# The last chunk's attention goes to layer 2's gates by a product of values and input weights

## The chip, the cores and the metric

One of the eight cores of a Trainium2 chip runs the kernel. The metric is the device time of one execution in microseconds; before the change it is 414.52 us (median of 3 runs, 414.26 to 414.95).

## The reference, cut to what matters

`x` is 16 x 128 x 128 (batch, time, features), `cond` 16 x 128. Two LSTM layers run over time with an attention without softmax between them and a feed-forward block behind them:

```python
hs = lstm(x, cond, Wx1, Wh1, b1)            # 128 steps; gates i, f, o sigmoid, g tanh
theta, phi, v = hs @ W_theta.T, hs @ W_phi.T, hs @ W_g.T
x = x + ((theta @ phi.T) / sqrt(128)) @ v   # over all 128 times of a batch row, no softmax
hs2 = lstm(x, cond, Wx2, Wh2, b2)           # 128 steps
x = x + relu(hs2 @ W1 + b1f) @ W2 + b2f
```

A step of an LSTM is `a = x_t @ Wx + b + h @ Wh`, `c = f*c + i*g`, `h = o*tanh(c)`. Layer 2's first step needs the attention's sum over all times, so it needs layer 1's last `h`.

## The kernel before, in words

The batch of 16 and 8 times make a chunk of 128 columns; there are 16 chunks (`NCH`), and a loop pass holds two (`STEPS` = 16 steps, `CH` = 8). Everything is kept with features on partitions. Each engine has its own instruction stream, written out by hand, with semaphores between; nothing is scheduled by a planner.

A step (function `step` of each engine): TensorE multiplies the last `h` (`ring`) with the f weights in f32 into `fbank` (L413), and the f16 high and low parts of `h` with two f16 parts of the g, i and o weights into `gbank`, `ibank` and `bankV` (L407). ScalarE makes the gates (f L818, g L825, i L828, o L833) and `tanh(c)` (L836). VectorE makes `f*c` (L1003), the scan that adds `i*g` (L1006), the o gate times a unit (L1013), then `h` as f32 into `ring` (L1016), its high part (L1018) and its low part (L1021). The input's and the bias's part of the gates stands in the same PSUM columns already: ScalarE copies the bias there (`seed`, L852) and TensorE adds `Wx` times the chunk (`project_gate`, L372) a chunk ahead, beside the steps. `bias_gate` (L367) does both for f.

Beside the steps each engine works off a list by the step's number (`beside1` in layer 1; in layer 2's first 16 steps the blocks `if s == ...`). In layer 1, `row_products` makes, from the 8 new times, keys' and values' rows (`rows`), SP's queue moves them by DMA into an order by batch row (`rows_t`, L277), and the attention of the first two chunks of queries is summed in `bankV` (`score_products` L477, mask by `keep_scores` L1028, `early_attention` L482). `fill` (L386) issues matmuls of no use that keep TensorE busy. The queries of chunks 2 to 15 come after layer 1: `outer_pair` (L610) makes keys times values of two batch rows, `attend_pair` (L623) multiplies it with the hidden states `hist_late`, and `late_x2` (L1109) adds x.

Between the layers: with the last `h` TensorE makes the score product, the values' rows and the keys' rows; ScalarE copies them; `early_attention` completes chunk 0, VectorE adds x (`early_x2`, L1034) to give `x2T[:, 0]`, and four projections give layer 2's gates of its first 8 steps. `initial` (L391) has added `h0` times `Wh2` for step 0 during layer 1's last chunk. Steps of layer 2 then follow, the first 16 written out on all engines, the rest in loops. TensorE and ScalarE have layer 1's last 16 steps written out; VectorE has them in its loop. All engines take their instructions in order, so a wait holds up everything behind it on that engine.

## Time and profile before

| | us |
|---|---|
| median of 3 runs | 414.52 |
| profiled execution | 414.66 |
| its span, first to last instruction | 412.7 |
| TensorE matmul busy | 392.8 (95%) |
| VectorE busy | 273.1 (66%) |
| ScalarE busy | 206.7 (50%) |
| TensorE weight load busy | 293.2 (71%) |
| chain of waits: TensorE, VectorE, ScalarE, issue | 68%, 17%, 9%, 4% of the span |

The profile is of one execution. PE is TensorE's matmul row, PEld its weight loads, DVE VectorE, ACT ScalarE, SPq the queue of SyncE. PE's busy share holds the fills, and matmuls overlap; it doesn't say that TensorE is the bound. The granted clock was 1.00 (2.4 GHz) over the whole span.

### The profile page before, as it was taken

The page shows a single profiled execution, that of the slowest core. Times are in us where ns is not written, and L with a number is a line of the kernel's source. Part 1 is how long each engine was busy: PE and PEld are TensorE (multiplying, and loading weights), DVE is VectorE, ACT ScalarE, POOL GpSimd, SP SyncE. Part 2 cuts the span into 40 slices and gives each one's busy share as a digit, 9 for nine tenths or more (in the row PEclk, how much of TensorE's full clock was granted, in tenths as well). Part 3 has the DMA queues.
Part 4 walks back from the last instruction along what each step waited for, and adds up shares of the span by engine and source line. Part 5 has one row for each costly group of instructions (what it writes and reads, how often), then busy time and mean ns, then how long its engine had stood idle before and what let it go on. Part 6 is the DMA issues. An engine that isn't in the chain of part 4 may idle for free.

```text
span 412.7 us, 14901 instructions
## 1 busy us (share of the span) xinstructions
PE 392.8 (95%) x4979; PEld 293.2 (71%) x4979; DVE 273.1 (66%) x1697; ACT 206.7 (50%) x1451; POOL 8.1 (2%) x20
## 2 busy tenths in 40 slices
PE   8999999999999999999999999999999999999996
PEld 6777666677666677666689877777777777777775
DVE  5676666665666666666668776666677666676664
ACT  3666555555544555544556444444444444444442
POOL 7000000000000000000000000000000000000000
PEclk9999999999999999999999999999999999999999
DMA  5111011111011111010000100000000000000000
GB/s 159 39 21 21 6 17 19 19 19 19 2 17 19 19 19 18 3 17 14 15 15 2 27 20 6 20 19 19 19 6 13 19 19 19 19 9 10 19 19 13
DMA packets 11697, 8.20 MB, mean 20 GB/s; under 512 B 1098, under 2 KB 11130, under 8 KB 11675
## 3 DMA queue, kind: packets, MB, share of 16 engines
q1 hardware_dynamic: 10842, 6.17, 7.5%
q0 software_dynamic: 544, 1.23, 1.0%
q10 hardware_dynamic: 288, 0.52, 0.4%
q8 instruction: 13, 0.21, 0.2%
q14 instruction: 10, 0.07, 0.1%
HBM read 2.87 MB, written 1.05 MB: 9 GB/s over the span
## 4 chain that ended last, share of the span: by engine, by line
PE 68%; DVE 17%; ACT 9%; issue 4%; DVEq 0%; ACTq 0%
PE fbank L413 22%; PE fbank L386 9%; DVE cell L1006 6%; DVE ring L1016 5%; ACT fgate L818 5%; DVE scan L1003 5%; ACT cell L836 5%; PE bankU L630 4%; PE bankV L407 4%; PE ibank L407 4%; PE gbank L407 3%; PE bankV L482 3%; PE bankY L637 2%; PE bankY L477 2%; PE bankU L515 2%
## 5 line engine op out<-in xcount | busy, mean ns | idle before, releaser
L413 PEld LDWEIGHTS fbank<-ring,whf 128*128 128x128 f32 x508 | 75.5, 188 | 77.9 <-DVE ring L1016 74.1
L386 PE MATMUL fbank<-warm_w 128*128 128x384 bf16 x537 | 125.2, 325 | 0.1
L818 ACT ACTIVATE fgate<-fbank 128x16 f32<-128x16 f32 x254 | 46.8, 184 | 139.3 <-PE fbank L413 138.9
L413 PE MATMUL fbank<-ring,whf 128*128 128x16 f32 x508 | 99.8, 272 | 15.1 <-DVE ring L1016 8.8
L1003 DVE TENSOR_TENSOR scan<-fgate,cell 128x16 f32<-128x16 f32 x254 | 43.7, 172 | 70.5 <-ACT fgate L818 61.1
L1016 DVE TENSOR_TENSOR ring<-cell,ogate_h 128x16 f32<-128x16 f32 x256 | 44.5, 174 | 41.7 <-ACT cell L836 41.3
L836 ACT ACTIVATE cell<-cell 128x16 f32<-128x16 f32 x256 | 43.0, 168 | 54.1 <-DVE cell L1006 53.9
L1006 DVE TENSOR_TENSOR_SCAN cell<-scan 128x32 f32<-128x32 f32 x256 | 59.4, 232 | 10.0 <-ACT scan L828 1.3
L407 PE MATMUL ibank<-h_hi,wh_parts 128*128 128x16 f16 x508 | 62.0, 169 | 0.0
L407 PEld LDWEIGHTS gbank<-h_hi,wh_parts 128*128 128x128 f16 x508 | 52.2, 137 | 0.0
L1021 DVE TENSOR_TENSOR h_lo<-ring,h_hi 128x16 f16<-128x16 f32 x256 | 44.9, 175 | 8.7
L386 PEld LDWEIGHTS fbank<-warm_w 128*128 128x128 bf16 x537 | 42.4, 97 | 10.0 <-issue 0.7
L407 PE MATMUL gbank<-h_hi,wh_parts 128*128 128x16 f16 x508 | 49.3, 169 | 0.0
L407 PE MATMUL gbank<-h_lo,wh_parts 128*128 128x16 f16 x508 | 49.3, 169 | 0.0
L407 PE MATMUL bankV<-h_hi,wh_parts 128*128 128x16 f16 x508 | 49.3, 169 | 0.0
L407 PE MATMUL bankV<-h_lo,wh_parts 128*128 128x16 f16 x508 | 49.3, 169 | 0.0
L407 PE MATMUL ibank<-h_lo,wh_parts 128*128 128x16 f16 x508 | 49.3, 169 | 0.0
L825 ACT ACTIVATE scan<-gbank 128x16 f32<-128x16 f32 x256 | 47.6, 186 | 1.2 <-PE gbank L372 1.2
L833 ACT ACTIVATE ogate<-bankV 128x16 f32<-128x16 f32 x256 | 47.1, 184 | 0.3 <-PE bankV L372 0.3
L828 ACT ACTIVATE scan<-ibank 128x16 f32<-128x16 f32 x256 | 46.4, 181 | 0.1
L407 PEld LDWEIGHTS ibank<-h_hi,wh_parts 128*128 128x128 f16 x508 | 43.4, 95 | 0.0
L1018 DVE TENSOR_TENSOR h_hi<-cell,ogate_h 128x16 f16<-128x16 f32 x256 | 42.0, 164 | 0.0
(189 smaller groups left out, 603.1 us busy)
## 6 DMA issues: line engine op xcount, KB each, us to landing
rows_t<-rows SPq DMA_DIRECT2D x16, 128.0 KB
x_rows<-in_x_dram SPq DMA_DIRECT2D x17, 64.0 KB
out_dram<-y_sb SPq DMA_DIRECT2D x16, 64.0 KB
xres<-x2T SPq DMA_DIRECT2D x15, 64.0 KB, 1.9
xin<-x2T SPq DMA_DIRECT2D x14, 64.0 KB, 1.8
w<-in_L_ffn_W_dram POOLq DMA_DIRECT2D x2, 256.0 KB, 4.0
wh<-in_L_cond_Wh_dram ACTq DMA_DIRECT2D x1, 256.0 KB, 3.0
wx<-in_L_cond_Wx_dram ACTq DMA_DIRECT2D x1, 256.0 KB, 3.5
```

The source lines that it names most:

```text
L386: nc.tensor.matmul(fbank[1 - p][:, P:4 * P], warm_w[:], warm_three, start=False, stop=True, skip_group_check=True)
L407: last = nc.tensor.matmul(step_out(p, t, g), wh_parts[layer][:, part, gate_cols(g)], h[:, (s - 1) % STEPS, :], start=False, stop=True, ski ...
L413: nc.tensor.matmul(step_out(p, t, GF), whf[layer][:], ring[:, (s - 1) % STEPS, :], start=False, stop=True, skip_group_check=True).then_inc ...
L818: nc.scalar.activation(fgate[:], fbank[p][:, NB * t:NB * t + NB], ACT.Sigmoid, scale=1.0 / Z_UNIT).then_inc(f_done[layer], 1)
L825: nc.scalar.activation(g_slots, shared_cols(p, GG)[:, NB * t:NB * t + NB], ACT.Tanh, scale=1.0 / Z_UNIT).then_inc(scan_inputs[layer], 1)
L828: nc.scalar.activation(i_slots, shared_cols(p, GI)[:, NB * t:NB * t + NB], ACT.Sigmoid, scale=1.0 / Z_UNIT).then_inc(scan_inputs[layer], 1)
L833: nc.scalar.activation(ogate[:], shared_cols(p, GO)[:, NB * t:NB * t + NB], ACT.Sigmoid, scale=1.0 / Z_UNIT).then_inc(o_done[layer], 1)
L836: nc.scalar.activation(tanhc, c_psum, ACT.Tanh).then_inc(h_inputs[layer], 1)
L1003: nc.vector.tensor_tensor(out=fc_slots, in0=fgate[:], in1=c_psum, op=ALU.mult).then_inc(scan_inputs[layer], 1)
L1006: nc.vector.tensor_tensor_scan(out=c_scan, data0=scan_mul, data1=scan_add, initial=0.0, op0=ALU.mult, op1=ALU.add).then_inc(c_ready[layer], 1)
L1016: nc.vector.tensor_tensor(out=ring[:, s, :], in0=tanhc, in1=ogate_h[:], op=ALU.mult).then_inc(h_ready[layer], 1)
L1021: nc.vector.tensor_tensor(out=h_lo[:, s, :], in0=ring[:, s, :], in1=h_hi[:, s, :], op=ALU.subtract).then_inc(lo_ready[layer], 1)
```

## The change

The sum of attention over chunks 0 to 14 for chunk 0's queries, with x, is formed beside step 14 of the last pass (`x2_base`, VectorE) and projected to g, i, f beside step 15 and to o after it. The last chunk's part no longer goes through the attention's output: beside steps 1 and 9 TensorE multiplies `wg_rows` with `Wx2` (`value_w`, scaled by VectorE after steps 3 and 11), and after the last step it makes `last_keys` times `value_w` for each gate (`gate_rows`, copied by ScalarE for g and o, by VectorE for i and f) and multiplies that with the masked scores straight into the gates (`attend_gate`). The complete `x2T[:, 0]`, the last chunk's rows and their DMA, the addition for chunk 1, the outer products, the late attention, and with them projections and feed-forward products move to later steps of layer 2. VectorE's last pass of layer 1 is written out.

```diff
@@ sync
-                sp.wait_ge(rows_kept, c + 3 + (c == NCH - 1))
+                sp.wait_ge(rows_kept, c + 3)
@@ tensor: step
+                if base_read:
+                    pe.wait_ge(base_kept, 1)
                 passes(h_hi, GO, (0, 1))
@@ tensor: beside1
+                before_last = isinstance(i, int) and i == ITER - 1
+                if before_last and t == 1:
+                    nc.tensor.matmul(bankY[:, 2 * P:4 * P], wg_rows[:], wx[1][:, 2 * P * p:2 * P * p + 2 * P],
+                                     start=True, stop=True).then_inc(value_w_ready, 1)
+                if before_last and t == 4:
+                    pe.wait_ge(value_w_kept, p + 1)
...
+                elif before_last and t == 1:
+                    fill(p, 1)
+                elif last and t >= 6:
+                    fill(p, 1)
                 else:
                     fill(p, FILL1[t])
                 if last:
                     fill(p, {2: 1, 3: 1, 4: 1}.get(t, 0))
-                    due = {3: (GG,), 5: (GI,), 7: (GO,)}
+                    due = {3: (GG,), 5: (GI,), 6: (GO,)}
...
-                    early_attention(rows[:, p, D:2 * D], 0, 0, 2 * P)
+                    attended = early_attention(rows[:, p, D:2 * D], 0, 0, 2 * P)
+                    if last:
+                        attended.then_inc(base_ready, 1)
+                if last and t == 7:
+                    project_gate(1, 0, GF, x2_base[:])
+                    fill(p, 1)
+                    pe.wait_ge(o_done[0], T)
+                    project_gate(1, 0, GG, x2_base[:])
+                    project_gate(1, 0, GI, x2_base[:])
@@ tensor: between the layers
+            def rows_of(g, out):
+                nc.tensor.matmul(out, last_keys, value_w[:, gate_cols(g)], start=True, stop=True
+                                 ).then_inc(gate_rows_ready, 1)
+            def attend_gate(g):
+                return nc.tensor.matmul(gate_out(0, g), gate_rows[:, g, :], scores[:, 0:P], start=False, stop=True,
+                                        skip_group_check=True)
             score_products(0, last_keys, 0, P).then_inc(scores_ready, 1)
-            nc.tensor.matmul(bankU[:, D:2 * D], last_keys, proj[:, 1, :], start=True, stop=True
-                             ).then_inc(rows_ready, 1)
-            nc.tensor.matmul(fbank[1][:, 0:D], last_keys, proj[:, 0, :], start=True, stop=True).then_inc(rows_ready, 1)
-            fill(1, 1)
-            pe.wait_ge(rows_kept, NCH + 2)
+            rows_of(GG, bankU[:, 0:P])
+            rows_of(GI, fbank[1][:, 0:P])
+            project_gate(1, 0, GO, x2_base[:])
             pe.wait_ge(scores_kept, NCH + 1)
-            early_attention(rows[:, 0, D:2 * D], 0, 0, P).then_inc(early_attn_ready, 1)
-            pe.wait_ge(rows_kept, NCH + 3)
+            rows_of(GO, bankY[:, 0:P])
+            pe.wait_ge(gate_rows_act, 1)
+            attend_gate(GG).then_inc(g_ready[1], 1)
+            rows_of(GF, bankU[:, 0:P])
+            pe.wait_ge(gate_rows_dve, 1)
+            attend_gate(GI).then_inc(i_ready[1], 1)
+            pe.wait_ge(gate_rows_act, 2)
+            attend_gate(GO).then_inc(o_ready[1], 1)
             bias_gate(1, 1, GF)
-            fill(1, 1)
-            pe.wait_ge(x2_first, 1)
-            project_gate(1, 0, GG, x2T[:, 0, :]).then_inc(g_ready[1], 1)
...
+            pe.wait_ge(gate_rows_dve, 2)
+            attend_gate(GF).then_inc(f_ready[1], 1)
@@ tensor: layer 2, first 16 steps
-                    step(1, s, s, x2_read=2 if s == 2 else None,
+                    step(1, s, s, x2_read={2: 1, 4: 2}.get(s),
                 if s == 0:
+                    row_products(1, bankY)
+                if s == 1:
                     nc.tensor.matmul(bankU[:, 0:D], hist[:, 0, :], proj[:, 1, :], start=True, stop=True
                                      ).then_inc(rows0_ready, 1)
+                    fill(0, 2)
+                    pe.wait_ge(rows_kept, NCH + 2)
+                    pe.wait_ge(o_done[1], 2)
+                    early_attention(rows[:, 0, D:2 * D], 0, 0, P).then_inc(early_attn_ready, 1)
+                if s == 2:
                     score_products(0, last_keys, P, P)
                     score_products(P, hist[:, 0, :], P, P).then_inc(scores_ready, 1)
+                    fill(0, 3)
+                if s == 3:
                     pe.wait_ge(rows0_kept, 1)
+                    pe.wait_ge(rows_moved[1], 16 * (ITER + 1))
+                    pe.wait_ge(rows_moved[0], 16 * (ITER + 2))
+                if 3 <= s < 3 + NB // 2:
+                    outer_pair(s - 3)
...
-                if 4 <= s < 4 + NB // 2:
-                    attend_pair(s - 4)
-                if s in (10, 11, 12):
-                    if s == 10:
+                if 5 <= s < 5 + NB // 2:
+                    attend_pair(s - 5)
+                if 4 <= s < 7:
+                    pe.wait_ge(seeded, 3 * NCH + 3)
+                    pe.wait_ge(o_done[1], s + 1)
+                    last = project_gate(1, 1, SEEDED[s - 4], x2T[:, 1, :])
+                if s in (11, 12):
+                    if s == 11:
                         pe.wait_ge(p_kept, NB // 2)
-                    for j in ((0,), (1,), (2, 3))[s - 10]:
+                    for j in ((0, 1), (2, 3))[s - 11]:
                         last = ffn_up(0, j)
                 if s == 13:
+                    pe.wait_ge(x2_done, NB // 2)
                     bias_gate(1, 0, GF)
-                    project_gate(1, 0, GF, x2T[:, 2, :])
-                fill(s // CH, {3: 1, 13: 1, 14: 1, 15: 2}.get(s, 0))
+                    fill(1, 2)
...
                     project_gate(1, 0, GG, x2T[:, 2, :])
                     project_gate(1, 0, GI, x2T[:, 2, :])
                 if s == 14:
+                    project_gate(1, 0, GF, x2T[:, 2, :])
                     residual(x2T[:, 0, :])
...
                     ffn_down(2)
                     ffn_down(3).then_inc(y_ready, 2)
+                    fill(1, 2)
+                    pe.wait_ge(o_done[1], 16)
+                    project_gate(1, 0, GO, x2T[:, 2, :]).then_inc(x2_projected, 1)
@@ scalar
-            nc.scalar.copy(rows[:, 0, D:2 * D], bankU[:, D:2 * D]).then_inc(rows_kept, 1)
-            nc.scalar.copy(rows[:, 0, 0:D], fbank[1][:, 0:D]).then_inc(rows_kept, 1)
+            nc.scalar.copy(gate_rows[:, GG, :], bankU[:, 0:P]).then_inc(gate_rows_act, 1)
+            nc.scalar.copy(gate_rows[:, GO, :], bankY[:, 0:P]).then_inc(gate_rows_act, 1)
             for s in range(STEPS):
                 step(1, s, s, opening=s == 0)
                 if s == 0:
+                    keep_rows(0, ITER, NCH)
+                if s == 2:
                     nc.scalar.copy(rows0[:], bankU[:, 0:D]).then_inc(rows0_kept, 1)
-                if 2 <= s < 2 + NB // 2:
+                if 3 <= s < 3 + NB // 2:
@@ vector
-            with dve.Fori(1, ITER) as i:
+            with dve.Fori(1, ITER - 1) as i:
...
+            for s in range(STEPS):
+                step(0, s, (ITER - 1) * STEPS + s)
+                beside1(ITER - 1, s)
+                if s % CH == 3:
+                    nc.vector.tensor_scalar(value_w[:, 2 * P * (s // CH):2 * P * (s // CH) + 2 * P],
+                                            bankY[:, 2 * P:4 * P], h_back(0), None, ALU.mult
+                                            ).then_inc(value_w_kept, 1)
+                if s == STEPS - 2:
+                    dve.wait_ge(base_ready, 1)
+                    nc.vector.scalar_tensor_tensor(out=x2_base[:], in0=xT[:, 0, :], scalar=1.0 / Z_UNIT,
+                                                   in1=bankV[:, 0:P], op0=ALU.mult, op1=ALU.add
+                                                   ).then_inc(base_kept, 1)
             keep_scores(P)
+            nc.vector.tensor_copy(gate_rows[:, GI, :], fbank[1][:, 0:P]).then_inc(gate_rows_dve, 1)
             nc.vector.memset(fc_slots, 0.0).then_inc(scan_inputs[1], 1)
-            early_x2(0)
+            nc.vector.tensor_copy(gate_rows[:, GF, :], bankU[:, 0:P]).then_inc(gate_rows_dve, 1)
                 if s == 0:
+                    keep_late(1, T - STEPS)
+                if s in (1, 3):
+                    early_x2(s // 2)
+                if s == 2:
                     keep_scores(2 * P)
-                if 4 <= s < 4 + NB // 2:
-                    late_x2(s - 4)
+                if 5 <= s < 5 + NB // 2:
+                    late_x2(s - 5)
```

## Rows read from the trace of the kernel before

**Rows 1.** Timeline, layer 1's last two steps: start, length, engine, line, output<-inputs, count

```profile
204.36 0.67 PE L482 MATMUL bankV<-scores,rows 128*128 128x256 f32 x2
204.63 0.17 DVE L1016 TENSOR_TENSOR ring<-cell,ogate_h 128x16 f32<-128x16 f32 x1 [0.16 <-ACT cell L836]
...
204.87 0.39 PE L413 MATMUL fbank<-ring,whf 128*128 128x16 f32 x2
...
205.28 0.12 PEld L407 LDWEIGHTS bankV<-h_hi,wh_parts 128*128 128x128 f16 x2
...
205.40 0.81 PE L386 MATMUL fbank<-warm_w 128*128 128x384 bf16 x4
...
205.58 0.18 ACT L833 ACTIVATE ogate<-bankV 128x16 f32<-128x16 f32 x1
...
206.18 0.17 DVE L1016 TENSOR_TENSOR ring<-cell,ogate_h 128x16 f32<-128x16 f32 x1 [0.16 <-ACT cell L836]
```

**Rows 2.** Timeline, the passage from layer 1 to layer 2

```profile
206.41 0.49 PE L477 MATMUL bankY<-queries,ring 128*128 128x128 f32 x2
...
206.73 0.39 PE L586 MATMUL bankU<-proj,ring 128*128 128x128 f32 x2
...
207.16 0.27 ACT L898 COPY rows<-bankU 128x128 f32<-128x128 f32 x1 [1.01 <-PE bankU L586]
...
209.31 0.23 DVE L1006 TENSOR_TENSOR_SCAN cell<-scan 128x32 f32<-128x32 f32 x1 [1.02 <-ACT scan L828]
...
209.78 0.17 DVE L1016 TENSOR_TENSOR ring<-cell,ogate_h 128x16 f32<-128x16 f32 x1
```

**Rows 3.** Timeline, layer 2, steps 1 to 3

```profile
211.32 0.17 DVE L1016 TENSOR_TENSOR ring<-cell,ogate_h 128x16 f32<-128x16 f32 x1 [0.16 <-ACT cell L836]
...
211.74 0.29 DVE L1034 SCALAR_TENSOR_TENSOR x2T<-xT,bankV 128x128 f32<-128x128 f32 x1
...
212.32 0.68 PE L610 MATMUL bankU<-rows_t 128*128 128x128 f32 x4
...
212.84 0.39 PE L372 MATMUL fbank<-x2T,wx 128*128 128x128 f32 x2
...
213.28 0.29 PE L413 MATMUL fbank<-ring,whf 128*128 128x16 f32 x2
...
214.50 0.17 DVE L1016 TENSOR_TENSOR ring<-cell,ogate_h 128x16 f32<-128x16 f32 x1 [0.17 <-ACT cell L836]
```

**Rows 4.** Timeline, layer 2, steps 9 and 10: late attention of two batch rows

```profile
223.83 0.17 DVE L1016 TENSOR_TENSOR ring<-cell,ogate_h 128x16 f32<-128x16 f32 x1 [0.16 <-ACT cell L836]
...
224.21 0.54 DVE L1109 SCALAR_TENSOR_TENSOR x2T<-xT,bankY 128x224 f32<-128x224 f32 x1
...
224.90 0.67 PE L623 MATMUL bankY<-hist_late,p_batch 128*128 128x112 f32 x4
```

**Rows 5.** Timeline, layer 2, steps 14 and 15: feed-forward

```profile
231.98 0.60 DVE L1123 TENSOR_SCALAR relu<-bankU,b 128x128 f32<-128x128 f32 x2
...
232.69 0.65 PE L637 MATMUL bankY<-w,relu 128*128 128x128 f32 x4
```

**Rows 6.** Timeline, ScalarE's copy of two chunks' rows in layer 1

```profile
198.31 0.38 ACT L842 COPY rows<-bankY 128x256 f32<-128x256 f32 x1
```

**Rows 7.** Last chunk's DMA: timeline; stretch: length, engines' busy, clock, DMA share, GB/s

```profile
207.67 0.61 SPq L277 DMA_DIRECT2D rows_t<-rows  x1
...
210.60:211.20 0.60, 0.51 (x7) 0.36 (x4) 0.51 (x4) 0.39 (x5) 0.00 (x0) 1.00 0.00 0
```

**Rows 8.** Layer 2's first back jump: timeline; DMA of 257:262, queue, packets, MB, share

```profile
257.97 0.17 DVE L1016 TENSOR_TENSOR ring<-cell,ogate_h 128x16 f32<-128x16 f32 x1 [0.16 <-ACT cell L836]
...
259.14 0.17 DVE L1003 TENSOR_TENSOR scan<-fgate,cell 128x16 f32<-128x16 f32 x1 [0.71 <-ACT fgate L818]
...
259.82 0.17 DVE L1016 TENSOR_TENSOR ring<-cell,ogate_h 128x16 f32<-128x16 f32 x1 [0.17 <-ACT cell L836]
...
q14 instruction: 1, 0.01, 0.5%
```

More of the change, by code:

```diff
@@ L121, in build @@
         rows0 = sb("rows0", [P, D])
+        value_w = sb("value_w", [P, 4 * H])
+        gate_rows = sb("gate_rows", [P, 4, H])
+        x2_base = sb("x2_base", [P, P])
         proj_at = sb("proj_at", [P, D])
@@ L205, in build @@
         rows0_ready = sem("rows0_ready")
+        value_w_ready = sem("value_w_ready")
+        value_w_kept = sem("value_w_kept")
+        base_ready = sem("base_ready")
+        base_kept = sem("base_kept")
+        gate_rows_ready = sem("gate_rows_ready")
+        gate_rows_act = sem("gate_rows_act")
+        gate_rows_dve = sem("gate_rows_dve")
         rows0_kept = sem("rows0_kept")
@@ L397, in top_product, with step @@
                 nc.tensor.matmul(out, ones[:], w_diag[:], start=True, stop=True).then_inc(top_ready[layer], 1)
-            def step(layer, s, count, o_parts=None, after_seeds={}, x2_read=None):
+            def step(layer, s, count, o_parts=None, after_seeds={}, x2_read=None, base_read=False):
                 p, t = s // CH, s % CH
@@ L577, in _ @@
             for s in range(STEPS):
-                step(0, s, (ITER - 1) * STEPS + s, after_seeds=seeds_before(NCH - 2 + s // CH, s % CH))
+                step(0, s, (ITER - 1) * STEPS + s, after_seeds=seeds_before(NCH - 2 + s // CH, s % CH),
+                     base_read=s == STEPS - 1)
                 if s == CH - 1:
@@ L656, in _ @@
                     pe.wait_ge(scores_kept, NCH + 2)
[L657 to L658 removed]
+                    pe.wait_ge(o_done[1], 4)
                     early_attention(rows[:, 0, D:2 * D], 0, P, P)
                     early_attention(rows0[:], P, P, P).then_inc(early_attn_ready, 1)
[L661 to L665 removed]
@@ L666, in _ @@
-                if s == 2:
-                    project_gate(1, 1, GF, x2T[:, 1, :])
-                if 4 <= s < 4 + NB // 2:
-                    attend_pair(s - 4)
-                if s in (10, 11, 12):
-                    if s == 10:
+                if s == 4:
+                    pe.wait_ge(x2_first, 2)
+                    project_gate(1, 1, GF, x2T[:, 1, :])
+                if 5 <= s < 5 + NB // 2:
[4 more added lines that the diff above has]
+                    last = project_gate(1, 1, SEEDED[s - 4], x2T[:, 1, :])
+                    if s == 6:
+                        last.then_inc(x2_projected, 1)
@@ L677, in _ @@
                 if s == 13:
+                    pe.wait_ge(x2_done, NB // 2)
                     bias_gate(1, 0, GF)
-                    project_gate(1, 0, GF, x2T[:, 2, :])
-                fill(s // CH, {3: 1, 13: 1, 14: 1, 15: 2}.get(s, 0))
-                if s in (2, 3):
-                    for g in ((GG,), (GI, GO))[s - 2]:
-                        pe.wait_ge(seeded, 3 * NCH + 2 * s - 3)
-                        pe.wait_ge(o_done[1], s + 1)
-                        last = project_gate(1, 1, g, x2T[:, 1, :])
-                    if s == 3:
-                        last.then_inc(x2_projected, 1)
-                if s == 12:
-                    pe.wait_ge(x2_done, NB // 2)
-                    pe.wait_ge(seeded, 3 * NCH + 5)
-                    pe.wait_ge(o_done[1], 13)
+                    fill(1, 2)
+                    pe.wait_ge(seeded, 3 * NCH + 6)
+                    pe.wait_ge(o_done[1], 14)
                     project_gate(1, 0, GG, x2T[:, 2, :])
                     project_gate(1, 0, GI, x2T[:, 2, :])
-                if s == 13:
-                    pe.wait_ge(seeded, 3 * NCH + 6)
-                    pe.wait_ge(o_done[1], 14)
-                    project_gate(1, 0, GO, x2T[:, 2, :]).then_inc(x2_projected, 1)
                 if s == 14:
+                    project_gate(1, 0, GF, x2T[:, 2, :])
                     residual(x2T[:, 0, :])
@@ L1040, in beside1 @@
                 p, t = s // CH, s % CH
-                if t == 5 and isinstance(i, int) and p == 0:
+                if t == 5 and isinstance(i, int) and i == 0 and p == 0:
                     dve.sem_inc(scores_kept, 1)
@@ L1045, in beside1 @@
                     keep_scores(2 * P)
-                if t == CH - 1 and (p == 0 or isinstance(i, int)):
-                    if isinstance(i, int):
-                        keep_first(p)
-                    else:
-                        keep_late(0, i * STEPS - CH)
-                if s == 0 and not isinstance(i, int):
+                first = isinstance(i, int) and i == 0
+                if t == CH - 1 and first:
+                    keep_first(p)
+                if t == CH - 1 and p == 0 and not first:
+                    keep_late(0, i * STEPS - CH)
+                if s == 0 and not first:
                     keep_late(1, i * STEPS - STEPS)
```

27 lines of the change are left out of this document (8 added, 19 removed).

## The prediction

> **What bounds the kernel now.** I read the page first, then the order of time around the places that the diff touches. The chain of waits is mostly TensorE, with VectorE and ScalarE in turn behind it (68% of the span, VectorE 17%, ScalarE 9%, by the page): no engine is simply full, the kernel is one long recurrence of 256 LSTM steps. In the timeline a step is the time from one write of `ring` to the next, 204.63 to 206.18, so 1.55 us [rows 1]. Counted from the write of `ring`: the f product starts at +0.24, the loads of the o products at +0.65, the first matmul of the work beside the step (here fills) at +0.77, the o gate's activation at +0.95, and the next `ring` comes at +1.55. What TensorE does beside a step is free only while it fits between +0.77 and the next f product. That one is due at 1.55 + 0.24 = +1.79; where TensorE runs without a break its weight load is already hidden and it may start some 0.1 later, so I take +1.88 as the deadline. A stretch of layer 2 checks this: behind the `ring` write at 211.32 TensorE does outer products and two projections, then the f product at 213.28, which is +1.96 and by this reckoning 0.08 late; from 211.32 to the `ring` write two steps on, 214.50, it is 3.18 us, and two steps of the beat are 3.10 [rows 3]. So whatever goes past +1.88 goes into the time nearly one for one.
>
> The exception to the beat is the passage from layer 1 to layer 2: `ring` at 206.18, next `ring` at 209.78, 3.60 us, 2.05 more than a step [rows 1, 2]. On it lie in series: score product, values' product, copy, attention product, addition to x, projections, then a step's tail. The change attacks this place, and pays in the steps around it.
>
> **Prices.** A first f32 product of 128 columns takes 0.32 (206.41 to 206.73), a following one 0.22 (two from 212.84 to 213.28), its result is there 0.39 to 0.49 after its start. A pair of them 0.52 (212.32 to 212.84). 256 columns: 0.43 following, 0.52 first (204.36 and its f product 0.51 later). A fill is about 0.16 (a last one ends 0.33 after its start; four 0.81 [rows 1]). A handover between engines is 0.04 to 0.06 (ring's end 206.35, product 206.41; product's end 207.12, copy 207.16). A 128-column copy on ScalarE is 0.27 [rows 2], the 128-column addition to x on VectorE 0.29 [rows 3].
>
> **Layer 1's last 16 steps.** Steps 1 and 9 trade three fills (0.48) for a product of 256 columns (0.52 with one fill behind it): +0.77 + 0.52 + 0.16 = +1.45, free. VectorE scales its 256 columns after steps 3 and 11; the 256-column row that I have on ScalarE is 0.38 [rows 6], I take 0.42, from +0.38 to +0.80, just ahead of VectorE's f multiplication. It moves TensorE's slot of steps 4 and 12 to about +0.90: 0.90 + 0.52 + 0.16 + 0.22 = +1.80, free, between 0 and +0.05 each. SP's queue sees nothing of this.
> In step 14 the o gate's initial product of layer 2 now stands ahead of the early attention, and both wait for the o activation. Before, the attention started at 204.36 (+1.28 from `ring` 203.08, one step ahead of 204.63) [rows 1]. The 16-column product ahead costs 0.23 (estimate: less than 0.32, more than 0.15), so the attention ends about 0.2 later, near 205.21, and the next f product is about 0.1 late. VectorE then adds x, 0.29, and is done at 205.54; the o products of step 15 wait for it (bankV is read by one and written by the other): their loads go from 205.28 to 205.60. The o activation goes to 205.90, its product with the unit ends near 206.28, and `ring` of step 15 is written at 206.32 instead of 206.18: **+0.14** (bounds +0.05, if the attention is not later, and +0.25). Step 15's slot starts at 205.72: fill, GF, fill, GG, GI = 0.16 + 0.22 + 0.16 + 0.22 + 0.22 = 0.98, so TensorE is free at 206.70, and against `ring`'s end plus hand-over (206.55, 206.65 with hidden load) another **+0.05**.
>
> **The passage.** Everything starts about 0.20 later than 206.41. Score product 206.70 (hidden load), result 207.09; rows for g 206.92, i 207.14; o's projection of the base 207.36. VectorE masks the scores 207.13 to 207.42, so the rows for o start at 207.58 at the latest. ScalarE copies g's rows (207.35 to 207.62): attended g starts at 207.80, rows for f 208.02, attended i 208.24 (its copy on VectorE, 207.57 to 207.86, is early), result 208.63. Activation and two handovers, 0.18 + 0.08, the scan at 208.89, and `ring` 0.47 behind the scan as before (209.31 to 209.78 [rows 2]): 209.36. **-0.42** for the two places together. The addition to x and one of two serial projections leave the path; in return TensorE has eight products where the path needs four, and the last of them (rows and attention of f) end only for step 1.
>
> **Layer 2's first 16 steps**, slot by slot, against +1.88:
> - Step 0 to 1: the row product of 256 columns starts at 209.12 and ends 0.6 later; ScalarE's copy of it (0.38 [rows 6]) runs to 210.14, while f's activation is due at 210.02. In order, so **+0.10** (0 to +0.15).
> - Step 1, 2, 3: 0.77 + 0.32 + 0.32 + 0.22; then, with the o products 0.11 late behind the addition to x (211.74 to 212.03, outer products only at 212.32 = +1.00, of which I give 0.12 to two more waits there [rows 3]), 0.89 + 0.54 + 0.48 = +1.91; then 0.88 + 0.52 + 0.44. Step 4 has the same sum as before's step 2 without its two extra waits. Before, these steps lost 0.01, 0.07 and 0.03 (the first two are the 0.08 above); now about 0.03 + 0.01 + 0.01: **-0.06**.
> - Steps 5 and 6: outer 0.52 + attend 0.40 + one projection 0.22 = +1.91: **+0.06** for both.
> - Steps 11 and 12: no outer product is left ahead of the attend pair, so the pair waits for the addition of the pair before, which starts 0.38 after `ring` and takes 0.54: with `ring` at 223.83 it stood at 224.21 and the pair at 224.90, +1.07 [rows 4]; it takes 0.50, by the 0.52 of a pair of 128 columns for its 112. Before, one up-product followed (+1.79, free). Now two: 1.07 + 0.50 + 0.44 = +2.01, **+0.13** each, +0.26.
> - Step 13: the wait for the last addition now stands at the head of the slot, with bias, two fills and two projections behind it: 1.07 + 0.32 + 0.32 + 0.44 = +2.15, **+0.26**. Before, it stood behind two up-products and was covered.
> - Step 14: 0.77 + 0.32 + 0.22 + 0.43, free.
> - Step 15: the relus (231.98, 0.60 for two, the same 0.38 after `ring`) end at 232.58, and the down products started 0.11 later [rows 5]. Before, two fills stood in the wait's shadow; now they stand behind it, and o's projection too: 1.10 + 0.53 + 0.33 + 0.22 = +2.18, **+0.30**.
> Sum here: 0.10 - 0.06 + 0.06 + 0.26 + 0.26 + 0.30 = +0.92. With -0.42: **+0.50**.
> - The DMA of the last chunk's rows moves from 207.67 to about 210.2. From 210.60 on nothing was moving any more [rows 7], so it landed in at most 3.0; now 213.2 at the latest, wanted at 213.4 (`ring` of step 2 at 212.63 plus 0.8). Cost 0, with little room. `x2_projected` comes later, but SP's queue waits ahead of it for the output of the first chunk, whose store is issued after that.
> - VectorE's loop of layer 1 runs six passes and a written-out seventh. Back jumps of that loop cost nothing in the trace. Layer 2's first back jump did: 1.85 from the `ring` write at 257.97 to the next at 259.82, with VectorE idle for 0.71 ahead of its f product at 259.14, and an instruction queue moved one packet in that stretch [rows 8]. That is 0.30 over the beat; the later ones show 1.57 or 1.58. VectorE's code ahead of this loop grows by 16 steps, so this may change either way; taken as unchanged, between -0.27 (gone) and +0.3 (a second one where the written-out part begins).
>
> The Trainium skill ("Runtime: NRT & Kernel Launch", Instruction fetch mechanics) says that instructions come in blocks of 16 KiB, two of them held, and that a taken branch whose target is in neither stalls on a fetch. By that rule the one packet at the back jump is such a fetch, and moving the loop against the blocks could remove the 0.3 or let it come back at each jump; that no later jump stalls agrees with it.
>
> **Rivals.**
> 1. The passage gains and the slots hide what I charge them: waits and fills overlap more than my sums say (deadline nearer +2.0, no loss in step 15 of layer 1). Then the passage gives 3.60 to 3.0, -0.6, the slots about +0.2, perhaps the stall's -0.27: 414.0. For it: products pipeline, and most slots lose nothing. Against: 213.28 shows the deadline, and [rows 4, 5] show both waits at the head of a slot.
> 2. Slots as charged and the stall at layer 2's first back jump gone: +0.50 - 0.27 = +0.23, 414.75.
> 3. Slower: the stall of rows 8 comes at each of the seven passes of layer 2's VectorE loop, since its body now lies badly: six more jumps at 0.27 = +1.6, time 416.7. It decides if VectorE's first instruction after a jump is again 0.3 behind f's activation. Against it: 256 steps of trace have only one such place.
> 4. Slower, smaller: the rows' DMA takes 0.5 longer than at most seen or is issued later; TensorE waits at step 3 of layer 2, +0.4, time 415.4.
>
> **The numbers.** The profiled execution took 414.66 (span 412.7 and 2.0 around it); plus 0.50 is 415.16. The median of the runs shown is 414.52, 0.14 lower, so I say 415.0. Chances: forecast 0.50, rival 1 0.20, rival 2 0.17, rival 3 0.06, rival 4 0.07. Medians of this kernel can tell about 0.2% (0.83 us) from nothing: 413.7 and 415.35 are the bounds. Faster gets 0.09 (rival 1's better half, with the stall gone too), slower 0.19 (rival 3, half of rival 4, the bad third of the forecast where several bounds add), the same 0.72. Range: rival 1 down to 413.8, and up to the forecast's upper bounds, 415.8; rival 3 lies outside.
>
> **What would show it.** Passage between the two `ring` writes about 3.04, with the write of step 15 near 0.14 late; steps 11, 12, 13 and 15 of layer 2 at 1.68, 1.68, 1.81 and 1.85, with TensorE never idle ahead of the f product; f's activation of step 1 directly behind ScalarE's 256-column copy; outer products of step 3 not waiting for the DMA. If these steps stay at 1.55 to 1.60 the forecast is wrong and the kernel is up to 0.6 faster. All other steps stay 1.55, granted clock full.

## The result and the profile after

The changed kernel takes 416.94 us (median of 6 runs, 415.69 to 418.9) against 414.5 (6 runs, 414.26 to 414.95): ratio 1.0061, interval 1.0048 to 1.0074. It is slower; I had said 415.0, no measurable change. By mean granted clock, five of the six executions have 0.991 to 0.996, and the one with 1.00 took 415.69.

In the timeline, the write of `ring` (rows L1063 now) gives the length of every step. What TensorE does beside step s runs past the `ring` write of step s - 1 and can delay the one of step s + 1, so "slot of step s" is the interval from the `ring` write of step s to the next. The intervals, each from two such rows, with what I had worked out; the last columns are another profiled execution of the same kernel (e12), where the clock stayed at 1.00, and e2, which has no late DMA:

```
interval                     before  forecast  after   e12    e2
step 14 to 15 of layer 1      1.55     1.69     1.73   1.72   1.72
passage to layer 2            3.60     3.04     3.05   3.06   3.06
layer 2: step 0 to 1          1.54     1.65     1.69   1.68   1.68
slots of steps 1, 2           3.18     3.14     3.10   3.10   3.10
slot of step 3                1.58     1.56     2.62   2.66   1.55
slot of step 4                1.55     1.56     2.49   1.59   1.56
slot of step 5                1.55     1.58     2.23   1.64   1.64
slot of step 6                1.55     1.58     1.64   1.64   1.64
slots of steps 11, 12         3.10     3.36     3.26   3.27   3.26
slots of steps 13, 15         3.11     3.66     3.52   3.52   3.51
step 14 of layer 1 to step 16 of layer 2
                             30.08    30.58    33.11  31.65  30.49
```

First, the timeline around the passage, which answers to [rows 1, 2]:

```profile
204.02 0.68 PE L494 MATMUL bankV<-scores,rows 128*128 128x256 f32 x2
...
204.74 0.29 DVE L1155 SCALAR_TENSOR_TENSOR x_base<-xT,bankV 128x128 f32<-128x128 f32 x1 [0.20 <-PE bankV L494]
...
205.80 0.17 DVE L1063 TENSOR_TENSOR ring<-cell,ogate_h 128x16 f32<-128x16 f32 x1
...
206.18 0.39 PE L489 MATMUL bankY<-queries,ring 128*128 128x128 f32 x2
...
206.83 0.27 ACT L943 COPY gate_rows<-bankU 128x128 f32<-128x128 f32 x1 [1.10 <-PE bankU L618]
...
207.74 0.39 PE L623 MATMUL ibank<-scores,gate_rows 128*128 128x128 f32 x2
...
208.38 0.23 DVE L1053 TENSOR_TENSOR_SCAN cell<-scan 128x32 f32<-128x32 f32 x1
...
208.85 0.17 DVE L1063 TENSOR_TENSOR ring<-cell,ogate_h 128x16 f32<-128x16 f32 x1
...
209.37 0.37 ACT L888 COPY rows<-bankY 128x256 f32<-128x256 f32 x1 [0.55 <-PE bankY L484]
...
209.64 0.19 ACT L864 ACTIVATE fgate<-fbank 128x16 f32<-128x16 f32 x1
...
209.77 0.61 SPq L287 DMA_DIRECT2D rows_t<-rows  x1
```

The passage went as worked out: `ring` of step 15 late by 0.18 (0.14 forecast), the scan 0.64 after the start of i's attention product, f's activation (209.64) directly behind the copy of 209.37. The new place is step 3 of layer 2. The timeline and, below it, the chain of waits (start, length, what):

```profile
213.64 0.17 DVE L1063 TENSOR_TENSOR ring<-cell,ogate_h 128x16 f32<-128x16 f32 x1 [0.17 <-ACT cell L882]
...
214.02 0.68 PE L651 MATMUL bankU<-rows_t 128*128 128x128 f32 x4 [1.01 <-DMA rows_t<-rows]
...
216.26 0.17 DVE L1063 TENSOR_TENSOR ring<-cell,ogate_h 128x16 f32<-128x16 f32 x1
...
218.75 0.17 DVE L1063 TENSOR_TENSOR ring<-cell,ogate_h 128x16 f32<-128x16 f32 x1 [0.16 <-ACT cell L882]
```

```profile
209.77 4.11 DMA rows_t<-rows
213.88 0.14 issue
214.02 0.68 PE bankU L651 x4
```

TensorE stood idle for 1.01 us: the DMA was issued at 209.77 and its semaphore came 4.11 later. In the kernel before they started at 212.32 [rows 3], 4.65 behind the issue at 207.67 [rows 7]; here TensorE was ready for them at about 213.0, only 3.2 behind it. The stretches show when the packets moved (columns: length, then busy time of PE, PEld, DVE, ACT, POOL, clock, DMA share, GB/s):

```profile
210.90:212.90 2.00, 2.00 (x35) 1.77 (x35) 1.56 (x9) 1.23 (x9) 0.00 (x0) 1.00 0.29 66
212.90:213.88 0.98, 0.11 (x5) 0.01 (x1) 0.71 (x5) 0.50 (x5) 0.00 (x0) 1.00 0.00 0
```

No packet started in the last 0.98 us before the semaphore. This is where [rows 7] misled me: they end with the last packet too. The trace of before also records the semaphore itself, which my reading left out (it is in the packed trace, not in these views): its eight updates run from 211.49 to 212.18, so the last came 4.51 us after the issue and 0.11 ahead of the outer products' weight load at 212.29. And behind the wait the clock fell, in this execution (first fence) and not in e12 (second):

```profile
215.00:216.00 1.00, 0.94 (x18) 0.85 (x17) 0.69 (x3) 0.66 (x5) 0.00 (x0) 0.90 0.00 0
216.00:217.00 1.00, 1.00 (x7) 1.00 (x7) 0.61 (x4) 0.41 (x3) 0.00 (x0) 0.50 0.00 0
217.00:218.00 1.00, 1.00 (x18) 1.00 (x17) 0.00 (x0) 0.28 (x3) 0.00 (x0) 0.50 0.00 0
218.00:219.00 1.00, 1.00 (x10) 1.00 (x8) 0.72 (x5) 0.52 (x5) 0.00 (x0) 0.50 0.00 0
219.00:220.00 1.00, 1.00 (x13) 1.00 (x13) 0.46 (x3) 0.37 (x1) 0.00 (x0) 0.90 0.00 0
```

```profile
215.00:216.00 1.00, 0.94 (x19) 0.85 (x18) 0.69 (x3) 0.67 (x5) 0.00 (x0) 1.00 0.00 0
216.00:217.00 1.00, 1.00 (x20) 1.00 (x19) 0.61 (x4) 0.60 (x4) 0.00 (x0) 1.00 0.00 0
```

0.50 is 1.2 GHz; by these five rows it lasted 3.4 us. TensorE reads as 1.00 busy in both, but issues 7 matmuls against 20 in the microsecond from 216: busy time doesn't show a slow clock, the count and the clock column do. The slots of steps 4 and 5, which nearly fit at 2.4 GHz (1.59 and 1.64 in e12), take 2.49 and 2.23.

### The profile page after: what moved, and what is told of

Same layout as the page of the kernel before. It is cut to its first block, busy times and chain, and to the rows that moved or that the text cites. A ratio compares the mean times of both kernels' runs of the same rounds, so it can differ in the third digit from the quotient of the medians.

```text
span 414.9 us, 14871 instructions
## 1 busy us (share of the span) xinstructions
PE 393.8 (95%) x4988; PEld 295.9 (71%) x4988; DVE 275.6 (66%) x1702; ACT 207.0 (50%) x1452; POOL 8.1 (2%) x20
## 4 chain that ended last, share of the span: by engine, by line
PE 67%; DVE 17%; ACT 9%; issue 4%; DMA 2%; DVEq 0%; ACTq 0%
PE fbank L423 21%; PE fbank L396 9%; DVE cell L1053 6%; ACT fgate L864 5%; DVE ring L1063 5%; DVE scan L1050 5%; ACT cell L882 4%; PE bankU L671 4%; PE bankV L417 4%; PE ibank L417 3%; PE gbank L417 3%; PE bankV L494 2%; PE bankY L678 2%; PE bankY L489 2%; PE bankU L527 2%
## 5 line engine op out<-in xcount | busy, mean ns | idle before, releaser
L396 PE MATMUL fbank<-warm_w 128*128 128x384 bf16 x528 | 122.9, 324 | 0.0
L1063 DVE TENSOR_TENSOR ring<-cell,ogate_h 128x16 f32<-128x16 f32 x256 | 44.6, 174 | 41.3 <-ACT cell L882 40.8
```

What stands on the lines that cost most here:

```text
L396: nc.tensor.matmul(fbank[1 - p][:, P:4 * P], warm_w[:], warm_three, start=False, stop=True, skip_group_check=True)
L1063: nc.vector.tensor_tensor(out=ring[:, s, :], in0=tanhc, in1=ogate_h[:], op=ALU.mult).then_inc(h_ready[layer], 1)
```

## The experiments

In the edits, `...` marks what is left out. Theory A: the change's own work costs what I forecast; the DMA wait adds 1.1 us to step 3, and the idle TensorE makes the clock fall, 1.5 us more. Rival B: steps 3 to 5 are overfull. Comparisons are with the kernel before on the same chip.

**e1, fills ahead of the wait.**

```diff
                 if s == 3:
+                    fill(0, 6)
                     pe.wait_ge(rows0_kept, 1)
```

> The changed kernel with six fills (0.97 us) ahead of TensorE's wait for the last rows' DMA in step 3 of layer 2; nothing else. Theory A (TensorE stood idle for 1.0 us at this wait, and the granted clock fell from 1.00 to 0.50 behind it): the DMA still sets step 3 (about 2.6 us from ring to ring), but TensorE is busy meanwhile, the clock stays at 1.00 and the next two steps fall from 2.49 and 2.23 to about 1.60: time about 415.2. Rival B (steps 4 and 5 are long because their slots hold too much work, the clock has its own reasons): these steps stay above 2.2 and the time stays at 416.8.

Measured: 415.49 (415.25 to 415.85, 8 runs), ratio 1.0027 (1.0017 to 1.0038), clock 1.00; slots of steps 3, 4 and 5: 2.68, 1.59, 1.64. The matmuls of no use, and the outer products behind them, in the timeline:

```profile
213.29 1.14 PE L396 MATMUL fbank<-warm_w 128*128 128x384 bf16 x6
...
214.48 0.52 PEld L651 LDWEIGHTS bankU<-rows_t 128*128 128x128 f32 x4 [0.45 <-issue]
```

B falls: steps 4 and 5 are fast once the clock holds. The wait itself is unchanged. The fills end at 214.43, so TensorE's matmul row is idle for 0.08 us ahead of the outer products (the 0.45 in the fence is idle time of its weight loads).

**e2, no late DMA.** (This kernel leaves out the last chunk's keys and values for the late queries: chunk 14's rows stand in their place.)

```diff
-            move_rows(NCH - 1, 0)
+            sp.wait_ge(rows_kept, NCH + 1)
+            sp.dma_start(rows_t[(NCH - 1) * CH:NCH * CH, :, :], rows[:, 1, :]).then_inc(rows_moved[1], 16)
...
-                    pe.wait_ge(rows_moved[1], 16 * (ITER + 1))
-                    pe.wait_ge(rows_moved[0], 16 * (ITER + 2))
+                    pe.wait_ge(rows_moved[1], 16 * (ITER + 2))
+                    pe.wait_ge(rows_moved[0], 16 * (ITER + 1))
```

> The changed kernel, but the last 8 partitions of the rows by batch row get chunk 14's rows once more (moved right behind chunk 14's own), instead of the last chunk's; so the late queries miss the last chunk's keys and values, and no DMA is late. Theory A: step 3 takes 1.56 instead of 2.62, steps 4 and 5 1.56 to 1.60 instead of 2.49 and 2.23, clock 1.00, time 416.9 - 2.6 = 414.3, below the kernel before. Rival B (overfull slots): steps 4 and 5 stay above 2.2, time 415.8 or more. My forecast on record had 415.0 for exactly this kernel.

Measured: 414.6 against 414.05, ratio 1.0009 (0.9999 to 1.0018). Slots 3 and 4 take 1.55 and 1.56. So the DMA's wait and the clock make nearly all of the loss. I had expected it below the kernel before, and it isn't. From step 14 of layer 1 to step 16 of layer 2 the profile has +0.41 (30.49 against 30.08) where +0.50 was forecast; behind it -0.39, by the back jumps (e3); from the first `ring` to the last both traces, before's and e2's, take 398.22. The medians differ by +0.55, the ratio says +0.4, give or take 0.4: nothing clear of noise.

**e3, one part of the change alone: VectorE's last pass of layer 1 written out in the kernel before.**

```diff
...
-            with dve.Fori(1, ITER) as i:
+            with dve.Fori(1, ITER - 1) as i:
                 for s in range(STEPS):
                     step(0, s, i * STEPS + s)
                     beside1(i, s)
+            for s in range(STEPS):
+                step(0, s, (ITER - 1) * STEPS + s)
+                beside1(ITER - 1, s)
```

> The kernel before with one part of the change alone: VectorE's last pass of layer 1 is written out. Theory (the 0.30 at layer 2's first back jump and 0.02 to 0.03 at each later one depend on where VectorE's loop lies): the step at the first back jump takes 1.56 instead of 1.85, the later ones 1.55 instead of 1.57 or 1.58, time 414.5 - 0.4 = 414.1. Rival (these 0.4 went by another part of the change, TensorE's or SP's): 414.5 and 1.85 as before.

Measured: 413.84 against 414.05, ratio 0.9990 (0.9981 to 1.0000). The interval at the first back jump, the answer to [rows 8], is 1.55:

```profile
257.80 0.17 DVE L1016 TENSOR_TENSOR ring<-cell,ogate_h 128x16 f32<-128x16 f32 x1 [0.16 <-ACT cell L836]
...
259.35 0.17 DVE L1016 TENSOR_TENSOR ring<-cell,ogate_h 128x16 f32<-128x16 f32 x1 [0.17 <-ACT cell L836]
```

and the later ones 1.55 instead of 1.57 or 1.58. From the first `ring` to the last the trace is 0.53 shorter (397.69), the medians say 0.2.

**e4, the changed kernel with other work in the shadow of the waits in steps 11, 12, 13 and 15.** (In 11 and 12 the up-products go ahead of the attend pair.)

```diff
+                if s in (11, 12):
...
                 if 5 <= s < 5 + NB // 2:
                     attend_pair(s - 5)
...
                 if s == 13:
+                    fill(1, 2)
                     pe.wait_ge(x2_done, NB // 2)
                     bias_gate(1, 0, GF)
-                    fill(1, 2)
...
                 if s == 15:
+                    fill(1, 2)
                     pe.wait_ge(relu_done, 4 + 4)
                     ffn_down(2)
                     ffn_down(3).then_inc(y_ready, 2)
-                    fill(1, 2)
```

> The changed kernel with TensorE's order altered in steps 11, 12, 13 and 15 of layer 2 alone: up-products ahead of the attend pair, fills ahead of the wait for the last addition, fills ahead of the wait for the relus. Theory (a wait at the head of a slot costs what stands behind it): the intervals of 1.71, 1.73 and 1.79 fall to 1.55 to 1.57, time 0.55 lower, 416.4, the DMA wait and the low clock untouched. Rival (TensorE's slots are simply too full there): no change, 416.9.

Measured: 416.18, but 414.6 to 418.51 over 10 runs, ratio 1.0050 (1.0030 to 1.0071); in the profiled one (414.6, clock 1.00) the slots of 11, 12, 13 and 15 take 1.55, 1.55, 1.56 and 1.55. Against 6.78 for these four in the changed kernel that is 0.57 less, by order alone. Five of the ten executions have a mean clock of 0.991 to 0.996 and took 416.13 to 418.35: here the clock fell. It doesn't explain all of the scatter: the longest, 418.51, has 1.00.

**e5, when does this DMA's semaphore come in the kernel before?**

```diff
                 if s == 1:
+                    pe.wait_ge(rows_moved[0], 16 * (ITER + 2))
                     pe.wait_ge(rows0_kept, 1)
```

> The kernel before with one wait added: TensorE waits for the last rows' DMA already at the head of step 1's slot in layer 2 (the DMA is issued at 207.67; that slot begins at 210.6). It measures when the semaphore of this DMA comes in the kernel before, where nothing showed it. Theory A (this DMA always needs some 4.1 us from issue to the waiting engine, about 1 us of it after its last packet; my 3.0 took the last packet for the landing): TensorE goes on at 211.8 and idles about 1.1 us. Rival C (in the changed kernel the DMA was slower by company, an instruction fetch and other traffic; here it lands by 210.7): TensorE goes on at 210.7 to 210.9, idle 0.1 to 0.3.

Measured (one run, 416.12), the DMA's issue and the first thing behind the wait, and then the chain's row:

```profile
207.86 0.61 SPq L277 DMA_DIRECT2D rows_t<-rows  x1
...
212.36 0.50 PE L386 MATMUL fbank<-warm_w 128*128 128x384 bf16 x2 [1.48 <-DMA rows_t<-rows]
```

```profile
207.86 4.45 DMA rows_t<-rows
```

4.45 us from issue to semaphore: C falls, the change didn't slow the DMA. In the kernel before it was even a little slower (4.51 in its own trace, 4.11 after) and came just in time. The last packet had ended at 210.39, 1.9 us ahead of the semaphore, so the 0.98 of the first comparison is no constant. The clock stayed at 1.00 here though TensorE idled for 1.5 us, which asked for e9.

**e6, the row product ahead of f's bias and attention.**

```diff
+            row_products(1, bankY)
             bias_gate(1, 1, GF)
             pe.wait_ge(gate_rows_dve, 2)
             attend_gate(GF).then_inc(f_ready[1], 1)
...
-                if s == 0:
-
-                    row_products(1, bankY)
```

> The changed kernel with one edit: the row product of the last chunk is issued ahead of f's bias and f's attention product in the passage, not behind them. Theory: ScalarE's copy starts at about 208.83 instead of 209.37, so f's activation of step 1 is not held up (ring to ring 1.56 instead of 1.69) and the DMA is issued 0.5 earlier: step 3 takes 2.2 to 2.3 instead of 2.62. Rival: bias and attention of f now end too late for step 1's f product, the gain of 0.13 is eaten, and the DMA wait shrinks all the same.

Measured (one run, 415.58): the DMA is issued 0.42 after step 0's `ring` instead of 0.92, step 0 to 1 takes 1.61 (1.69), step 3's slot 2.18 (2.62). The wait shrinks by what the issue is earlier. Of the 0.14 that step 0 to 1 had lost, 0.08 came back. The rival gave a reason for the rest: f's bias and attention now stand directly ahead of the f product of step 1 (209.57 and 209.90 in the timeline); no run separates it.

**e7, e4 and e6 together, early attention ahead of the DMA's wait.**

```diff
                 if s == 3:
                     pe.wait_ge(rows0_kept, 1)
+                    pe.wait_ge(scores_kept, NCH + 2)
+                    fill(0, 1)
+                    pe.wait_ge(o_done[1], 4)
+                    early_attention(rows[:, 0, D:2 * D], 0, P, P)
+                    early_attention(rows0[:], P, P, P).then_inc(early_attn_ready, 1)
                     pe.wait_ge(rows_moved[1], 16 * (ITER + 1))
...
```

> The edits of e4 and e6 together, and in step 3 the early attention stands ahead of the wait for the DMA, the outer products behind it. Theory: the semaphore (issue at about 209.2 plus 4.1) comes at 213.3, before the early attention has ended at 213.7; no wait is left, the outer products make step 3 about 0.2 too long (1.75), the clock stays at 1.00 in every execution: 0.9 below e4's undisturbed 414.6, that is 413.7 where the kernel before has 414.05. Rival: the early attention waits for the o activation, this costs 0.5 or more in step 3, and the time is that of the kernel before or above.

Measured: 414.26 against 414.29, ratio 1.0000 (0.9990 to 1.0009), no scatter (413.89 to 414.82). The rival was nearer: no wait for the DMA is left, yet step 3's slot takes 2.00, not 1.75, as two products behind the o activation and two behind those make it end late. The order is at fault: e2 has the same four products, the outer ones first, in 1.55.

**e8, the outer products one step later.** (The wait for the DMA now stands in step 4. The up-products stand ahead of the attend pair in steps 12 and 13, and step 13's two fills are gone. `initial(1, GO)` is back in layer 1's step 15 instead of a fill, which moved to step 14.)

```diff
-                if 3 <= s < 3 + NB // 2:
-                    outer_pair(s - 3)
+                if 4 <= s < 4 + NB // 2:
+                    outer_pair(s - 4)
...
-                if s in (11, 12):
+                if s in (12, 13):
...
-                    due = {3: (GG,), 5: (GI,), 6: (GO,)}
+                    due = {3: (GG,), 5: (GI,)}
...
+                    initial(1, GO)
```

> As e7, but the outer products stand one step later (steps 4 to 11, the attend pairs stay), the up-products in steps 12 and 13, and in layer 1's last steps o's initial product goes back from step 14 to step 15, in the place of a fill. Theory: step 3 takes 1.55, the DMA has 1.5 us of room, step 15 of layer 1 falls from 1.73 to 1.60: 0.3 below e7, 413.4 against 414.05 for the kernel before, ratio 0.998. Rival (slots 5, 6, 12 and 13 now each hold more than fits): 0.2 or more is given back there and it is no faster than e7.

Measured: 413.74 (413.48 to 414.42, 11 runs) against 414.29, ratio 0.9985 (0.9976 to 0.9994): faster than the kernel before. But part of the change had given that much by itself: e3, VectorE's pass written out and nothing else, has 0.9990 (0.9981 to 1.0000), and from the first `ring` to the last both traces, e3's and this one's, take 397.69. So the passage's gain here just pays for the slots; a gain beyond e3's isn't shown. Step 3's slot is 1.56. Slots 5 and 6 stay at 1.64 and 13 at 1.64, so a quarter of a microsecond is left there. Step 15 fell from 1.73 to 1.56, but the passage rose from 3.05 to 3.21: together 4.78 before and 4.77 now. That o product had only moved from one side of the `ring` write to the other.

**e9, e5's kernel over more executions.** Same edit.

> The kernel of e5 again (before, with TensorE's wait for the DMA at the head of step 1's slot, 1.57 us idle), now timed over many executions. In the changed kernel five of six executions had a clock below 1.00; in e5's single one it stayed 1.00. Theory A (standing idle for a microsecond or more behind a long busy stretch puts the clock at risk, whatever kernel it is): executions scatter, some 1.5 to 4 us above the lowest, as with e4. Rival D (the clock falls for something else in the changed kernel, its denser steps of f32 products): all executions within 0.8 us of 415.9, as with e1.

Measured: 416.39 (415.8 to 418.11, 4 runs), ratio 1.0046 (1.0029 to 1.0063). The profiled one had the fallen clock:

```profile
206.00:212.00 6.00, 4.50 (x43) 3.68 (x43) 3.05 (x17) 2.50 (x14) 0.00 (x0) 1.00 0.13 26
212.00:214.00 2.00, 1.97 (x23) 1.88 (x22) 1.16 (x7) 0.92 (x6) 0.00 (x0) 0.63 0.00 0
214.00:216.00 2.00, 2.00 (x22) 2.00 (x21) 0.49 (x4) 0.86 (x5) 0.00 (x0) 0.50 0.00 0
216.00:218.00 2.00, 2.00 (x13) 1.94 (x12) 0.55 (x5) 0.54 (x2) 0.00 (x0) 0.50 0.00 0
218.00:220.00 2.00, 2.00 (x27) 2.00 (x28) 0.95 (x7) 1.03 (x6) 0.00 (x0) 0.66 0.00 0
```

Its steps behind the wait took 2.62, 2.77 and 2.01; e5's took 1.58, 1.58, 1.55. By the mean clocks it fell in two of the four executions (0.992 and 0.996; the others 1.00), and not in e5. D falls: the kernel before loses its clock too, once TensorE idles at this place, and only in some executions.

**e10 and e11, VectorE's code made longer in the kernel before** (3 and 7 per step).

```diff
             for s in range(STEPS):
                 step(1, s, s, opening=s == 0)
+                for _ in range(3):
+                    dve.sem_inc(unused, 1)
```

> The kernel before with 48 more instructions on VectorE's sequencer (3 semaphore increments that nobody waits for in each of layer 2's first 16 steps); no work. It asks what took away the 0.30 at layer 2's first back jump in e3. By my count of the instruction streams VectorE's layer-2 loop is instructions 419 to 579; here 467 to 627. Block theory (the stall comes when the loop body lies across a block border near instruction 512): the interval at the first back jump stays near 1.85. Rival (any shift changes it, or only the written-out pass does): it falls to 1.55, or e11 shows 1.85 too.

> As e10 with 112 instructions more: VectorE's layer-2 loop is now instructions 531 to 691, wholly behind 512, as in e3 (519 to 679). Block theory: the interval at the first back jump is 1.55 to 1.58 and the later ones 1.55. Rival (only writing out the pass did it): 1.85. The first 16 steps of layer 2 may be a few hundredths longer each, by VectorE's sequencer.

Measured (one run each, 418.28 and 422.58; the first 16 steps of layer 2 grew by 3.7 and 8.3 us, far more than I thought): the interval at the first back jump is 1.56 with 48 more and 1.55 with 112 more, later ones 1.55. My border at 512 is wrong, since 48 more left the loop across it (by my count of instructions). What holds is that each of three shifts (48, 100 in e3, 112) removed the 0.30 and the 0.02 after it; why is open.

Both runs also lost their clock, from about 228.7 (e10) and 231.0 (e11) on and for 6.8 us, which is part of their growth. TensorE had no wait there as long as the changed kernel's in step 3. The waits in e10, and its stretches:

```profile
226.34 0.67 PE L624 MATMUL bankY<-hist_late,p_batch 128*128 128x112 f32 x4 [0.38 <-DVE x2T L1110]
...
228.09 0.67 PE L624 MATMUL bankY<-hist_late,p_batch 128*128 128x112 f32 x4 [0.40 <-DVE x2T L1110]
```

```profile
226.00:228.00 2.00, 1.35 (x20) 1.28 (x20) 1.63 (x9) 0.83 (x8) 0.00 (x0) 1.00 0.00 0
228.00:230.00 2.00, 1.91 (x22) 1.94 (x23) 1.55 (x9) 1.03 (x7) 0.00 (x0) 0.66 0.00 0
230.00:232.00 2.00, 2.00 (x20) 2.00 (x20) 0.64 (x5) 0.40 (x3) 0.00 (x0) 0.50 0.14 41
```

Two waits of 0.38 and 0.40 in successive steps stood ahead of the fall, in e11 two of 0.73. So no single wait of 1 us is needed. Each of these runs is one execution.

**e12, the changed kernel again.**

> The changed kernel unaltered, on the chip of e9. Theory A: executions scatter from 415.4 (clock 1.00 throughout) to 419 (fallen), lowest about 0.9 above e1's rank against the kernel before; the median ratio is again about 1.006. Rival (the slow clock was the first chip's): the ratio is 1.003 with little scatter, the DMA wait alone.

Measured: 415.5 (median of 9, 415.2 to 417.4 but for one of 475.25 with a mean clock of 0.561, which the ratio leaves out; nothing on record says why that one was slow), ratio 1.0036 (1.0022 to 1.0050). Six of the nine have a mean clock of 1.00, one 0.999 and one 0.996, so here the kernel costs mostly the DMA's wait and the slots, and the first comparison's 1.0061 holds the fallen clock of five of six executions. How often it falls is not the kernel's alone.

## Why the prediction was wrong

- **The step that failed** is the term of the DMA, put at nothing: "so it landed in at most 3.0 [...] Cost 0, with little room". From the stretch in which nothing moved I had concluded that the data had landed and the engine could know it. The semaphore came 4.11 us after the issue, and in the other traces 4.10 to 4.51: 4.51 already in the kernel before, where it was 0.11 ahead of need. How far it came behind the last packet varied from 0.5 us (e6) to 2.0 (before), so the packets don't tell it. It cost 1.1 us in step 3 (2.66 in e12 against 1.55 in e2; between medians, e1 less e2, 0.9). The Trainium skill ("DMA: Bandwidth & Descriptors", Anatomy of one DMA — SWDGE (gpsimd) path) says that the semaphore can't fire before the last byte's write is confirmed in the target memory, and puts most of the fixed 2 us of a DMA by gpsimd's path there. This DMA goes by SP's queue; its traces agree in kind, with 0.5 to 2.0 us from the last packet to the semaphore. I had not weighed this rule, and it spoke against the change.
- **Rival 4** named the place and gave 0.4; it was 1.1, and it missed what follows. I had written "granted clock full". The clock fell behind the idle in the profiled execution, worth 1.5 us (slots 4 and 5: 4.72 against 3.23 in e12), and by the mean clocks in four of the other five. e1 shows that fills hold it, in eight executions of eight, where on the same chip e4, with the idle left in, lost it in five of ten. The wait for the DMA is as long in e1, so it is the idle TensorE and not the length of the step. e9 shows that the kernel before loses it at the same idle. Why only some executions lose it is open.
- **The passage** was right: 3.05 measured, 3.04 worked out; with step 15 it gained 0.37 (0.42 forecast). It rested on 0.22 for a following f32 product and on the copies' order.
- **The deadline of +1.88** held. Step 11 was 0.16 late (0.13 forecast), step 13 0.18 (0.26), step 15 0.24 (0.30), steps 5 and 6 0.09 each (0.03; in e12 the f product of the first stood at +2.01, not +1.91). In slot 11, after:

```profile
227.28 0.17 DVE L1063 TENSOR_TENSOR ring<-cell,ogate_h 128x16 f32<-128x16 f32 x1 [0.16 <-ACT cell L882]
...
228.36 0.67 PE L664 MATMUL bankY<-hist_late,p_batch 128*128 128x112 f32 x4 [0.16 <-DVE x2T L1171]
...
228.86 0.62 PE L671 MATMUL bankU<-ring,w 128*128 128x128 f32 x4
...
229.32 0.29 PE L423 MATMUL fbank<-ring,whf 128*128 128x16 f32 x2
```

  The f product is at +2.04 from 227.28, 0.16 behind +1.88. Step 12, forecast 0.13, lost nothing: its wait counts from the `ring` write before the late one, its deadline from the late one, so of two slots in a row that begin with such a wait only the first paid. That was an error of mine in the sum. It doesn't hold for slots that are full without a wait: steps 5 and 6 both paid.
- **Layer 2's first back jump** no longer stalls: rival 2's -0.27 came (e3), and 0.02 at each later one, which I had not counted. The cause isn't shown, and the instruction packet of [rows 8] isn't what VectorE waited for: in that trace it started at 259.46, and VectorE had gone on at 259.14.
- **The sum** without DMA and clock was +0.50. In e2's trace the same places give +0.41, where errors of both signs cancel: steps 5, 6 and step 0 to 1 cost 0.16 more than I had, steps 11 to 15 cost 0.25 less. The back jumps give -0.39 besides; by its ratio e2 is -0.04 to +0.75 from the kernel before.

## What to carry to other kernels

When a DMA is moved later, time it from issue to the engine that waits; the last packet doesn't tell (here the semaphore came 0.5 to 2.0 us behind it). When nobody waited in the trace of before, look up the semaphore's last update there, or put a wait in and measure it. In a kernel whose beat depends on TensorE's clock, a wait is worth its length and the risk of the clock: put fills or other work ahead of it. In a full slot, what must wait goes behind what needn't: e4 won 0.57 us with no instruction less. And run each part of a change alone: the part that moved VectorE's loop (e3) accounts for the whole gain of the best kernel here (e8).

## What the runs showed of the hardware

- An SBUF-to-SBUF DMA of 128 KB in rows of 1 KB, from SP's queue: first packet 1.25 us after the issue's start in all ten traces that I compared, last packet 2.5 us after it (before, e1, e4, e5, e9, e12) or 3.1 to 3.7 (after, e6, e7, e8), semaphore 4.10 to 4.23 in the changed kernels and 4.45 to 4.51 in the kernel before.
- TensorE idle for 1.0 to 1.5 us behind a long busy stretch: in some executions the granted clock fell from 1.00 to 0.50 within 2 us of the idle's end, and in others of the same kernel it stayed (after and e12; e5 and e9). It was down for 3.4 us in the changed kernel and for 6.8 in e9. With fills in the wait and 0.08 idle it stayed in 8 executions (e1). With waits of 0.4 us in two successive steps it fell in one (e10).
- Semaphore increments that nobody waits for are dear on VectorE between steps: while the clock was at 1.00, 3 in a step lengthened it by 0.17 (e10) and 7 by 0.53 (e11), so 0.06 to 0.08 us each.
- A stall of 0.30 at a back jump of VectorE's loop went away with 48 instructions more ahead of it.
